# Cross attention with another turn-taking in its transposing bank, and fp8 attention with its normed input in the bank of the probabilities

## What is computed

```python
x = _layernorm(x + linear_attention(x))
# cross attention: 16 query heads, 4 key heads of 128; keys of the context and of x: 256 keys
q = rope(rms_norm((x @ Wq.T).reshape(.., 16, 128), q_norm_w))
k = rope(rms_norm((concat([context, x]) @ Wk.T).reshape(.., 4, 128), k_norm_w))
v = (concat([context, x]) @ Wv.T).reshape(.., 4, 128)
x = _layernorm(x + (softmax(q @ k.T * SCALE) @ v) @ Wo.T)
x = _layernorm(x + bit_linear(rms_norm(silu(gate(x)) * up(x)), w_down))      # int8 MLP, 256 -> 1024 -> 256
x = _layernorm(x + state_space(x))
# fp8 attention: h is normed, each stream rounded to fp8; 16 query heads twice, 8 key heads
h = _ln(x, ln_w, ln_b)
core = gqa(_ln(fp8(h) @ wq), _ln(fp8(h) @ wk), fp8(h) @ wv)
xout = gqa(_ln(fp8(h) @ wqx), _ln(context @ w_kx), context @ w_vx)
x = _layernorm(x + fp8(concat([core, xout])) @ wproj)
x = _layernorm(x + quantized_linear(x, weight))
```

## Time and profile before

| | us |
|---|---|
| median of 3 runs | 2226.64 (2224.39 to 2228.84) |
| the profiled execution's own time | 2222.77 |
| its span, first to last instruction | 2221.0 |
| PE busy | 2025.4 (91%) |
| DVE busy | 1655.2 (75%) |
| ACT busy | 1330.0 (60%) |
| POOL busy | 1264.5 (57%) |

### The profile page before, as it was taken

The page is one execution under the profiler, slowest core; times in us unless marked ns, Lnnn a source line. Parts: engine busy times, 40 slices in busy tenths (PEclk is TensorE's granted clock), DMA queues, the critical chain, the costliest instruction groups (busy, mean ns, idle before and its releaser), DMA issues.

```text
span 2221.0 us, 35586 instructions
## 1 busy us (share of the span) xinstructions
PE 2025.4 (91%) x10014; PEld 1332.0 (60%) x10116; DVE 1655.2 (75%) x3833; ACT 1330.0 (60%) x5022; POOL 1264.5 (57%) x1550
## 2 busy tenths in 40 slices
PE   7879999999999998899999967999999999999995
PEld 4646666656666655565565534666666666666664
DVE  7755666667767667688888845778888887877886
ACT  3655666665666665334334216777777777777773
POOL 0054344445444442477777743777777777777775
PEclk9999999999999999999999978999999999999998
DMA  6000000000000002100000011000000000000000
GB/s 221 1 17 6 3 4 3 2 5 2 2 2 2 2 0 82 67 10 19 29 20 10 1 34 50 6 3 6 6 6 5 6 5 6 5 8 6 3 3 8
DMA packets 30094, 37.62 MB, mean 17 GB/s; under 512 B 3328, under 2 KB 24320, under 8 KB 29312
## 3 DMA queue, kind: packets, MB, share of 16 engines
q1 hardware_dynamic: 29952, 36.11, 4.8%
HBM read 34.00 MB, written 2.10 MB: 16 GB/s over the span
## 4 chain that ended last, share of the span: by engine, by line
PE 59%; DVE 17%; ACT 10%; issue 6%; POOL 6%; DMA 0%; SPq 0%; DVEq 0%; POOLq 0%; ACTq 0%
PE xa_pJB L736 6%; PE xa_pS L755 5%; PE fa_pJB L1906 5%; PE xa_pO L829 5%; PE xa_pY L859 5%; PE xa_pJA L736 4%; PE fa_pS L1925 4%; PE fa_pY L1956 3%; PE fa_pO L1943 3%; PE fa_pJA L1886 3%; PE fa_pH L2007 2%; POOL ssm_y L1347 2%; PE fa_pJB L1886 2%; ACT fa_k_junk L2026 2%; POOL fa_rs L1842 2%
## 5 line engine op out<-in xcount | busy, mean ns | idle before, releaser
L1842 POOL TENSOR_TENSOR fa_rs<-fa_rs,all_minus_half 128x4 f32<-128x4 f32 x192 | 198.2, 1032 | 15.1
L2033 ACT ACTIVATE fa_qT<-fa_pH,all_fa_head_vec 128x512 f32<-128x512 f32 x128 | 99.5, 777 | 172.2 <-PE fa_pH L2007 172.2
L1347 POOL TENSOR_TENSOR ssm_y<-ssm_y,ssm_term 128x512 f32<-128x512 f32 x112 | 141.9, 1267 | 82.1 <-DVE ssm_term L1615 79.4
L2042 ACT ACTIVATE fa_pS<-fa_pS,fa_nb 128x128 f32<-128x128 f32 x512 | 182.6, 392 | 6.9 <-issue 6.5
L1839 POOL TENSOR_TENSOR fa_rs<-fa_ms,all_eps5w 128x4 f32<-128x4 f32 x192 | 43.9, 229 | 239.8 <-ACT fa_q_junk L2026 132.3
L1925 PEld LDWEIGHTS fa_pS<-fa_kT,fa_qT 128*128 128x128 f32 x1024 | 124.7, 192 | 65.4 <-ACT fa_qT L2033 58.5
L682 POOL TENSOR_TENSOR xa_rs<-xa_ms,all_eps 128x4 f32<-128x4 f32 (+1 forms) x65 | 13.2, 202 | 259.0 <-ACT xa_junk L904 259.0
L1865 POOL TENSOR_TENSOR fa_cat<-fa_ov,fa_om 128x512 bf16<-128x512 f32 x128 | 153.7, 1201 | 5.3
L1925 PE MATMUL fa_pS<-fa_kT,fa_qT 128*128 128x128 f32 x1024 | 149.0, 289 | 2.5 <-ACT fa_qT L2033 0.9
L1856 POOL TENSOR_TENSOR fa_ov<-fa_ob,fa_om 128x512 f32<-128x512 bf16 x128 | 147.7, 1154 | 4.7 <-DVE fa_om L2220 4.7
L755 PE MATMUL xa_pS<-all_shared_weights,xa_qT 128*128 128x256 f32 x512 | 125.8, 387 | 23.3 <-ACT all_shared_weights L935 17.5
(11 more groups left out here) (330 smaller groups left out, 5918.3 us busy)
## 6 DMA issues: line engine op xcount, KB each, us to landing
all_shared_weights<-in_fa_w SPq DMA_DIRECT2D x12, 512.0 KB, 3.7
fa_cat<-in_fa_wproj SPq DMA_DIRECT2D x8, 512.0 KB, 3.7
all_shared_weights<-in_xa_wq SPq DMA_DIRECT2D x1, 2048.0 KB, 13.8
xa_wo<-in_xa_wo SPq DMA_DIRECT2D x1, 2048.0 KB, 17.7
xa_ctxT<-in_ctxT SPq DMA_DIRECT2D x16, 128.0 KB, 2.1
all_shared_weights<-in_fa_wkvx SPq DMA_DIRECT2D x1, 2048.0 KB, 9.8
fa_ctxT<-in_ctxT SPq DMA_DIRECT2D x16, 128.0 KB, 2.1
out_x<-all_X SPq DMA_DIRECT2D x16, 128.0 KB, 1.7
```

The lines of the kernel that those rows point to most:

```text
L1347: pool.tensor_tensor(y[:, side, :], y[:, side, :], term[:, in_turn(side, l), :], ALU.add)\
L1842: pool.tensor_tensor(rs[:, j % 2, cols], rs[:, j % 2, cols], env.mhalf[:, cols], ALU.pow)\
L2042: last = act.activation(four(pS[j % 2])[:, i, :], four(pS[j % 2])[:, i, :], ACT.Exp, bias=nb[:, j % 2, i:i + 1], accum_out=rsum[:, j % 2, ...
```

## The change

In cross attention the transposes in `pH` change their turns, on TensorE and on ScalarE alike. The queries of step `j + 1` are transposed near the beginning of step `j`, behind the probabilities (instead of those of step `j + 2` at the end). The next row's x is transposed behind the scores of step 0, the next row's keys at the end of steps 1 and 2, behind the output product. On ScalarE the copy to `qT` stands between the two pairs of exponentials, the copy of x behind the MLP's `hqT` copy, the copy of keys ahead of the silu of the second half, and the MLP's square behind the squares of the queries. In fp8 attention `xn` is transposed into `pP`, the bank of the transposed probabilities, behind the key projection of step 1, and its copy to `lnT` stands behind the copy to `qT`. There the keys of step 1 don't wait for `lnT` any more; the transposes of the probabilities in step 2 do. VectorE's `norm.vector_apply` and `tnorm.vector_stats` move from step 5 to step 6, GpSimd's `tnorm.pool_rstd` from the end of step 6 to step 7.

```diff
@@ -759,21 +759,16 @@
-
-                if front and j == 0:
-                    pe.wait_ge(s["cur_in"], at(m + 1, 0, 1))
...
-                keys = front and j > 1 and OTHERS[j - 2][0] == "k"
-                if keys:
-                    pe.wait_ge(kk["scaled"], at(m + 1, j - 2, 2))
-                    pe.wait_ge(q["T_in"], at(m, j + 1))
...
+                if there(j + 1):
+                    pe.wait_ge(q["roped"], at(m, j + 1))
+                    pe.wait_ge(q["T_in"], at(m, j))
+                    if front and j == 1:
+                        pe.wait_ge(s["xT_in"], at(m + 1, 0, 1))
+                    if front and j > 1:
+                        pe.wait_ge(kk["T_in"], at(m + 1, j - 2, 2))
+                    for h in range(HG):
+                        last = pe.transpose(pH[:, h * P:(h + 1) * P], qr[:, (j + 1) % 2, h, :], env.ident[:])
+                    last.then_inc(q["T_ps"], 1)
                 if there(j + 3):
@@ -811,6 +806,12 @@
                         scores(n, to, b)
+                if front and j == 0:
+                    pe.wait_ge(s["cur_in"], at(m + 1, 0, 1))
+                    pe.wait_ge(q["T_in"], at(m, j + 1))
+                    for k in range(KT):
+                        last = pe.transpose(pH[:, k * P:(k + 1) * P], cur[:, k * P:(k + 1) * P], env.ident[:])
+                    last.then_inc(s["xT_ps"], 1)
                 if there(j - 2):
@@ -860,6 +861,13 @@
                         last.then_inc(s["y_ps"], 1)
+                if front and j > 0 and OTHERS[j - 1][0] == "k":
+                    pe.wait_ge(kk["scaled"], at(m + 1, j - 1, 2))
+                    pe.wait_ge(q["T_in"], at(m, j + 1))
+                    for g in range(G):
+                        last = pe.transpose(pH[:, g * P:(g + 1) * P], kn[:, OTHERS[j - 1][1], g, :],
+                                            env.ident[:])
+                    last.then_inc(kk["T_ps"], 1)
                 if end and j == 0:
@@ -880,16 +888,6 @@
                         .then_inc(fh["gate_ps" if j == 1 else "up_ps"], 1)
-                if there(j + 2):
-                    pe.wait_ge(q["roped"], at(m, j + 2))
-                    pe.wait_ge(q["T_in"], at(m, j + 1))
-                    if front and j == 0:
-                        pe.wait_ge(s["xT_in"], at(m + 1, 0, 1))
-                    if keys:
-                        pe.wait_ge(kk["T_in"], at(m + 1, j - 2, 2))
...
@@ -913,35 +911,35 @@
             for j in js:
-                if there(j):
-                    act.wait_ge(a["bias"], at(m, j))
-                    act.wait_ge(a["p1_ps"], at(m, j) - 2)
-                    for h in range(HG):
...
-                        if h % 2:
-                            last.then_inc(exp_done, 1)
-                if mid and j == 3:
...
-                if front and j == 0:
...
-                if front and j > 1 and OTHERS[j - 2][0] == "k":
-                    act.wait_ge(kk["T_ps"], at(m + 1, j - 2, 2))
...
+                for b in range(2):
+                    if there(j):
+                        if b == 0:
+                            act.wait_ge(a["bias"], at(m, j))
+                            act.wait_ge(a["p1_ps"], at(m, j) - 2)
+                        for h in (2 * b, 2 * b + 1):
+                            last = act.activation(pr[:, j % 2, h, :], pS[b][:, (h % 2) * NK:(h % 2 + 1) * NK],
+                                                  ACT.Exp, bias=nb[:, j % 2, h:h + 1],
+                                                  scale=rs[:, (j + 2) % G, h:h + 1],
+                                                  accum_out=rsum[:, j % 2, h:h + 1])
+                        last.then_inc(exp_done, 1)
+                    if b == 0 and there(j + 1):
+                        act.wait_ge(q["T_ps"], at(m, j + 1))
+                        act.activation(qT[:, (j + 1) % 2, :, :], heads(pH), ACT.Copy).then_inc(q["T_in"], 1)
                 if there(j - 1):
...
                     square(pJA, junk[:, 0], ms[:, (j + 1) % G, 0:HG], q["ps"], at(m, j + 3), q["squared"])
+                if mid and j == 3:
+                    act.wait_ge(fh["hid_done"], now(m - 2, 0, 2, 1))
+                    act.activation(hq[:], hid[:], ACT.Square, scale=1.0 / float(np.sqrt(I)), accum_out=hms[:])\
+                        .then_inc(f["squared"], 1)
                 if end and j == 0:
...
                     act.activation(hqT, pJB[:, :].bitcast(BF16), ACT.Copy).then_inc(f["hqT_in"], 1)
+                if front and j == 0:
+                    act.wait_ge(s["xT_ps"], at(m + 1, 0, 1))
+                    act.activation(xT[:, 1 - side, :], pH[:, 0:D], ACT.Copy).then_inc(s["xT_in"], 1)
                 if mid and j == 1:
@@ -959,11 +957,12 @@
                     act.activation(xqT[:], pO[:, :].bitcast(BF16)[:, 0:D], ACT.Copy).then_inc(f["xqT_in"], 1)
+                if front and j > 0 and OTHERS[j - 1][0] == "k":
+                    act.wait_ge(kk["T_ps"], at(m + 1, j - 1, 2))
+                    act.activation(kT[:, 1 - side, OTHERS[j - 1][1], :, :], heads(pH), ACT.Copy)\
+                        .then_inc(kk["T_in"], 1)
                 if mid and j == 1:
                     silu(m - 2, pO, 1)
-                if there(j + 2):
-                    act.wait_ge(q["T_ps"], at(m, j + 2))
-                    act.activation(qT[:, (j + 2) % 2, :, :], heads(pH), ACT.Copy).then_inc(q["T_in"], 1)
@@ -1850,6 +1849,8 @@
                     rstd(q, slice(0, HG), j, at(m, j + 2))
+                if last_linear and j == 7:
+                    tnorm.pool_rstd(pool, m - 2, 0)
                 if there(j - 3):
@@ -1870,8 +1871,6 @@
                     norm.pool_rstd(pool, m - 1, 0)
-                if last_linear and j == 6:
-                    tnorm.pool_rstd(pool, m - 2, 0)
@@ -1929,6 +1928,8 @@
                     pe.wait_ge(a["pT_in"], at(m, j - 1) - 1)
+                    if front and j == 2:
+                        pe.wait_ge(s["lnT_in"], at(m + 1, 0, 1))
                     for i in range(HG):
@@ -1959,18 +1960,10 @@
-                if front and j == 1:
-                    pe.wait_ge(s["xn_done"], at(m + 1, 0, 1))
-                    pe.wait_ge(q["T_in"], at(m, j + 1))
-                    for k in range(KT):
-                        last = pe.transpose(pH[:, k * P:(k + 1) * P], xn[:, k * P:(k + 1) * P], env.ident[:])
-                    last.then_inc(s["xn_ps"], 1)
                 if keys:
...
                     pe.wait_ge(q["T_in"], at(m, j + 1))
-                    if j == 1:
-                        pe.wait_ge(s["lnT_in"], at(m + 1, 0, 1))
                     for i in range(HG):
@@ -1993,6 +1986,13 @@
                     other(m + 1, 1 - side, *OTHERS[j])
+                if front and j == 1:
+                    pe.wait_ge(s["xn_done"], at(m + 1, 0, 1))
+                    if attend:
+                        pe.wait_ge(a["pT_in"], at(m, 0))
+                    for k in range(KT):
+                        last = pe.transpose(pP[:, k * P:(k + 1) * P], xn[:, k * P:(k + 1) * P], env.ident[:])
+                    last.then_inc(s["xn_ps"], 1)
                 if there(j + 2):
@@ -2046,12 +2046,6 @@
                     act.activation(pT[:, (j - 1) % 2], four(pP), ACT.Copy).then_inc(a["pT_in"], 1)
-                if front and j == 1:
-                    act.wait_ge(s["xn_ps"], at(m + 1, 0, 1))
...
                 if front and j > 0 and OTHERS[j - 1][0] == "k":
@@ -2062,6 +2056,12 @@
                     head_in(q, qT[:, n % 2], 0 if n < 4 else 4, m, j + 2, UNITS)
+                if front and j == 1:
+                    act.wait_ge(s["xn_ps"], at(m + 1, 0, 1))
+                    for k in range(KT):
+                        last = act.activation(lnT[:, k, :], pP[:, k * P:(k + 1) * P], ACT.Identity,
+                                              bias=vec[:, k, 1:2], scale=vec[:, k, 0:1])
+                    last.then_inc(s["lnT_in"], 1)
                 if front:
@@ -2228,9 +2228,9 @@
                                       w_proj[:, 0, 4 * j:4 * j + 4, :], ALU.subtract).then_inc(wp_low, 1)
-                if back and j == 5:
+                if back and j == 6:
                     norm.vector_apply(dve, m - 1, 0)
-                if last_linear and j == 5:
+                if last_linear and j == 6:
                     tnorm.vector_stats(dve, m - 2, 0)
...
                     tnorm.vector_apply(dve, m - 2, 0)
```

26 lines of the change are left out of this document (removed).

## The result

The changed kernel takes **2189.1 us** (median of 4 runs, 2187.53 to 2189.35) against 2227.5 (2224.39 to 2228.84) for the kernel before: ratio 0.9828, 95% interval 0.9811 to 0.9845. Its profiled execution took 2188.9, against 2222.8: 33.9 us less, and the forecast was 34.3. Against the medians it is 38.4 less, so the gain is told as 34 to 38 us.

A forecast was written before the change was run, and what follows sets the result against it. TensorE's program in its order bounds the kernel, so only its waits can be won: cross attention 20.8 + 2.5 and fp8 attention 8.5 + 2.5 sum to 34.3 us, making 2192 us, range 2177 to 2209.

The forecast's parts named there:

- The new wait at step 2: Cross attention, scores of step 2: TensorE waits 1.10 us for ScalarE's chain of keys copy, silu, table load, exponentials, `qT` copy.
- `hq`: Cross attention, transposes of the MLP's `hq`: TensorE comes earlier and waits 0.4 us for VectorE's list, 0.1 to 0.8 as ends.
- the two bank waits: Cross attention, bank `pH`, keys to queries: a wait of some 0.05 us, twice a unit, with the MLP as cover.
- the 1.65 of the earlier trace: Cross attention, scores of step 3: a 1.65 us wait for the keys, behind ScalarE's MLP square and copy, is won.
- the early units: Units 0 to 2, an estimated gain of 2.5 us in cross attention and 2.5 us in fp8 attention.
- the squares come 0.24 earlier: fp8 attention, step 2: ScalarE's squares of the keys start 0.24 us earlier, so that much is won a unit.
- 0.41 for the norms: fp8 attention, step 6: with VectorE's norms a step later, the keys' scaling starts earlier, winning 0.41 us a unit.
- The waits are only handed on: Rival, chance 0.17: `hq` and table load cost their ends, 0.8 and 1.5, fp8 step 1 gives nothing; 18 us, 2208.
- the new waits don't stand: Rival, chance 0.12: ScalarE reaches silu earlier and `hq` is in time; 50 us gained, 2176.
- Nothing moves: Rival, chance 0.03: the bank's turns were no limit, TensorE waits for the softmax chain all the same; 2226.
- slower: Rival, chance 0.05: scores behind the `qT` copy make the softmax loop longer than a step; 12 us slower, 2238.
- the drain: Rival, chance 0.03: a drain at the table load costs 1.38 us more a unit, 18 us less gained; 2210.

The follow-up runs named there:

- the two later traces: Traces of the kernel before with only the change's cross attention part (2199.8 us) and with only its moved fp8 norms (2224.3 us); filling 79.8 and 79.9 us.

## Why the prediction was right, and where its terms were off

**Cross attention, right in its steps.** The waits for `kT` and for the copies are gone (3.20 a unit). The new wait at step 2 was put at 1.10 and is 0.95; `hq` at 0.4, is 0.27; the two bank waits at 0.05 each, are 0.07. That the chain of step 2 is the cause is shown from both sides: taking the chain's start forward removed the 0.95, and putting `qT` behind the exponentials made it 2.04. The square is another matter: the forecast read the 1.65 of the earlier trace rows as the square and the copy behind it, but the move of the square wasn't needed; put back, it costs 0.1 a unit. Measured 2.05 a unit, forecast 1.60. Of the 0.45 between, 0.24 lies in the three new waits; the rest is small waits of before that the forecast didn't list (some 0.1 each ahead of step 1's key projection and between it and `Y` among them). For the early units I added 2.5. By the distances between output products units 0 and 1 won 1.18 and 0.72, twelve full units 24.5 and the last 0.87; against that 1.3 us were lost in the filling, which the forecast had at nothing. In four traces with this order of cross attention the first output product came 0.6 to 3.2 us later behind the stage's start than before; what it waits for there wasn't pursued.

**fp8 attention, right in sum by luck, wrong in the split.** Forecast 0.65 a unit, measured 0.60, but no unit has either: seven of the twelve full ones won 0.95, the five behind the branch 0.12. I had read one unit, at 1846, which stands behind the loop's branch, and took it for all. The step "the squares come 0.24 earlier" is right there (0.24) and undersized in every second unit (0.51). The step "0.41 for the norms" is right inside an iteration (0.42): the wait ahead of step 6's keys fell from 0.70 to 0.25 in both kinds of unit. It is wrong behind the branch, where VectorE's later norms stand ahead of 2.4 to 2.7 us in which it issues nothing, and the new wait for `qn` takes back more than that (0.1 to 0.2 lost). The two errors cancel. For the early units I added 2.5: units 0 and 1 won 1.3, and in the filling 2.1 were won against the two later traces, 0.4 lost against the one that I had read. The forecast looked for a cost of the later norms in step 7 ("some 0.1"); it is at the branch, in step 0.

**The total.** Up to the state-space stage 25.9 us were won for a forecast of 23.3, in fp8 attention 7.9 for 11.0. That the sum, 33.9 in the profiled executions, met 34.3 so closely is luck: the two differences cancel, and by the medians 38.4 were won.

**The rivals.** "The waits are only handed on" and "the new waits don't stand" were each half there, in small: the new waits stand at 0.95 and 0.27. "Nothing moves" and "slower" fell with the unit of 45.7. For the drain, ScalarE: Activation LUTs of the Trainium skill, What ACT_TABLE_LOAD costs, gives some 1380 ns of a drain on top of the load at each switch of set. After the change the load starts at 518.58, 0.02 behind the silu's end, and the exponential at 519.87, 0.01 behind the load's end: the trace doesn't agree, and no such rival was at work.

## What to carry to other kernels

A bank shared by several transposes made each of them wait for the copy of the one before; give each a turn where the emptying engine comes by soon, and then move the producers ahead of work that is wanted later (here `Y`), which won 16.8 us with no instruction changed. Read two units running before multiplying by their number: the loop body of two units has two kinds here. Where an engine's list has no gap behind a branch, another order of two of its instructions won nothing; that work taken off the list would help is likely, but no run here tried it. And take a second trace of the same kernel before splitting a gain by stages: the filling alone differed by 2.5 us here.
